# Scatter-add in place of a weighted combine: a mixture-of-experts layer behind latent attention

## The chip, the cores and the metric

The kernel runs on one core of a Trainium2 chip. A core has five engines with queues of their own: TensorE (PE in the profile, its weight loads PEld), VectorE (DVE), ScalarE (ACT), GpSimd (POOL) and SyncE (SP), and 16 DMA engines that move data for all of them. The metric is the device time of one execution in microseconds, as the median of several runs.

## The reference

The input is 8 sequences of 1024 tokens with 256 channels. One attention block with 16 heads comes first, then a layer norm; its result is `x1` (8192 tokens). Then a mixture of 8 experts with two of them chosen for each token, a residual, and two layer norms in a row:

```
gates = softmax(x1 @ gate_w); topw, topi = top_k(gates, 2); topw = topw / sum(topw)
h = gelu(LN(x1 @ w1[e] + b1[e]) * ln1_g[e] + ln1_b[e]);  y[e] = h @ w2[e] + b2[e]
out = LN(sum_e combine[e] * y[e] + x1) * ln_g + ln_b
result = LN(x1 + out)
```

For two chosen experts the normalised weights are 1/(1+exp(d)) and exp(d)/(1+exp(d)), with d the second logit less the first.

## The kernel before

**Attention phase** (`attention_phase`). It is cut into 32 units (8 sequences by 4 groups of heads). Each unit's steps carry places on one axis (the table `PLACES`, 24 places a unit), and every engine runs its own steps sorted by place; so the table is the order of all five queues. At the end of a sequence come the steps that matter here. `STORE` (L410-412) writes the 1024 rows of x1 from the SBUF array `z` to DRAM from SP's queue. `R` is the routing: 22 small DVE steps (`route_step`, L605-650) on 8 columns of tokens, each waiting for the one before; step 12 leaves the difference of the two logits in an array `weight`. `CNT` counts on PE. `SCAT` (L805-811) is 16 indirect DMAs from POOL that write, for every token and choice, a pair of integers into the table `token_of_row`: the token, and the row of `y_rows` that the result goes to.

The last sequence's tail runs in a block of its own together with the loading and splitting of the expert weights. There DVE works out, from the counts, the table of tiles (which expert, which first row), and at its end both gate weights of all tokens (L945-949, with an exponential on ACT, L902).

**Expert phase** (`expert_phase`). There are 136 tiles of 128 rows. All engines run a software pipeline over the tile number k. SP loads the table rows of a tile into `tok` (16 slots). POOL's loop has three steps (L1011-1029): the gather of x1 rows for tile k+6 (L1017), the power -0.5 of the variance for tile k+2 (L1023), and the scatter of the results of tile k-2 (L1028), which puts each row, unweighted, into its own row of `y_rows`. PE transposes, multiplies by w1 and w2 in split precision, ACT applies the gelu and copies the result out of PSUM (L1118), DVE does the normalisation. Rows that pad a tile gather token 0 and scatter to rows of their own behind the results.

**Combine phase** (`combine_phase`). There are 16 groups of 4 tiles of 128 tokens. SP loads three arrays for each group, x1 and the two results y0 and y1, in three rotating buffers each, and stores the output (L1218-1230). ACT builds for each tile two 128x128 diagonal matrices that hold the gate weights (L1337). PE makes f = x1 + w0 y0 + w1 y1 with one identity product and two diagonal ones (L1243, L1245), and x1 + ln_b in a second set (L1254, L1255). DVE takes moments of f, makes 1/sqrt from ACT's square root by a reciprocal and one Newton step (`invert`), forms v = (f - mean) rstd g + (x1 + b) in two passes (L1289, L1295), takes moments of v; ACT applies the last norm (L1354).

## Time and profile before

| what | value |
| --- | --- |
| runs | 2346.51, 2357.85 and 2376.85 us; median 2357.85 |
| span of the profiled execution | 2336.8 us (9.7 below the lowest run shown) |
| busy share of the span | PE 90%, DVE 74%, ACT 58%, POOL 56% |
| expert phase | 1665 to 2172 us of the span, 136 tiles |
| combine phase | 2172 to 2337 us of the span, 16 groups |
| mean granted TensorE clock | 0.94 of full speed |

The span runs from the first to the last instruction of the core; a run's time also holds what lies before and behind it. Busy shares are averages over phases with different limits, so each phase is read by itself. A row of a timeline or a line gives the duration of one instruction; consecutive instructions of one engine overlap a little, so that the distance between starts is the better measure of a series. "idle before <- X" names who ended the wait before an instruction, and "issue" an idle time in which the profile shows no one waited for.

### The profile page before, as it was taken

How to read it: one execution, taken by the hardware profiler on the slowest of the kernel's cores; microseconds unless marked ns; L12 is line 12 of the kernel's file. 1: busy time of each engine (PE TensorE's matmuls, PEld its weight loads, DVE VectorE, ACT ScalarE, POOL GpSimd, SP SyncE). 2: the span in 40 equal slices, each digit the busy share in tenths (PEclk: the TensorE clock that was granted, in tenths of full speed). 3: DMA queues.
4: the chain of work that ended last, by engine and by line, in shares of the span. 5: the costliest groups of instructions: out<-in, count | busy, mean ns of one | idle time of the engine just before them, and what ended most of it. 6: DMA issues, size and time to landing. Idle time of an engine off the chain costs nothing. (4 is left out here: it accounts for less than half of the span.)

```text
span 2336.8 us, 43530 instructions
## 1 busy us (share of the span) xinstructions
PE 2092.7 (90%) x12268; PEld 1464.7 (63%) x12268; DVE 1721.4 (74%) x4995; ACT 1365.5 (58%) x3316; POOL 1308.8 (56%) x1478
## 2 busy tenths in 40 slices
PE   4898999899899899899999999983399999999698
PEld 3554655555555555465556555642399999999587
DVE  3676687677678668668767767836488888888498
ACT  1265655655565565565555556563288887888454
POOL 2355464654764665666465476454577777777000
PEclk7899998999999999999889899995699999999899
DMA  6556556546565554655654556515122222222575
GB/s 176 127 135 142 118 115 149 126 106 150 127 135 128 135 122 118 156 118 116 149 123 109 140 124 146 115 39 213 26 74 74 76 75 76 74 74 69 182 243 168
DMA packets 190406, 284.46 MB, mean 122 GB/s; under 512 B 54072, under 2 KB 111056, under 8 KB 190032
## 3 DMA queue, kind: packets, MB, share of 16 engines
q1 hardware_dynamic: 168608, 236.43, 42.7%
q0 software_dynamic: 17152, 35.81, 5.0%
q10 hardware_dynamic: 4416, 9.44, 1.1%
q8 instruction: 110, 1.80, 0.3%
q14 instruction: 120, 0.98, 0.1%
HBM read 100.03 MB, written 37.90 MB: 59 GB/s over the span
## 5 line engine op out<-in xcount | busy, mean ns | idle before, releaser
L544 ACT ACTIVATE probs<-scores_T 128x512 f32<-128x512 f32 (+3 forms) x1536 | 654.4, 492 | 243.8 <-PE scores_T L433 240.7
L783 POOL TENSOR_SCALAR_AFFINE_SELECT probs<-probs 128x256 f32<-128x256 f32 x512 | 205.7, 410 | 522.4 <-ACT probs L544 519.4
L492 PE MATMUL ring<-k_stack,q_stack_b 96*128 96x512 f32 (+3 forms) x1024 | 396.3, 429 | 22.1 <-DVE neg_part L691 10.4
L691 DVE TENSOR_REDUCE neg_part<-ring 128x1 f32<-128x512 f32 x512 | 333.6, 685 | 97.6 <-PE ring L492 95.6
L433 PE MATMUL scores_T<-q_stack_b,k_stack 98*128 98x512 f32 (+3 forms) x1024 | 318.1, 387 | 45.4 <-ACT probs L544 44.5
L450 PE MATMUL o_ps<-probs,v_ones 128*17 128x512 f32 (+3 forms) x3072 | 341.8, 518 | 2.1 <-POOL probs L783 1.8
L492 PEld LDWEIGHTS ring<-k_stack,q_stack_b 96*128 96x128 f32 x1024 | 192.3, 196 | 227.4 <-issue 72.6
L696 DVE CUSTOM_DVE_ANT_0 ring<-ring,mask 128x384 f32<-128x384 f32 (+3 forms) x512 | 243.6, 508 | 113.5 <-PE ring L492 111.4
L696 DVE CUSTOM_DVE_ANT_0 ring<-ring,mask,neg_part 128x384 f32<-128x384 f32 (+3 forms) x512 | 260.5, 555 | 63.5 <-PE ring L492 63.3
L1107 ACT ACTIVATE o_sb<-ht_ps,ln_b,ln_g 128x128 f32<-128x128 f32 x544 | 217.9, 450 | 87.1 <-PE ht_ps L1056 86.6
L433 PEld LDWEIGHTS scores_T<-q_stack_b,k_stack 98*128 98x128 f32 x1024 | 186.3, 198 | 99.6 <-ACT probs L544 78.6
L552 ACT ACTIVATE u<-ring,lat_bias 128x512 f32<-128x512 f32 x128 | 88.0, 689 | 190.7 <-PE ring L474 178.5
L474 PE MATMUL ring<-x_hi,lat_w 128*128 128x512 f32 x512 | 188.4, 410 | 8.1 <-DMA lat_w<-lat_split 8.1
L492 PE MATMUL ring<-k_stack,q_stack_a 96*128 96x384 f32 (+3 forms) x512 | 170.9, 367 | 25.5 <-DMA k_stack<-u_rot 20.8
L760 POOL TENSOR_TENSOR u<-u,cos 128x512 f32<-128x512 f32 x126 | 162.2, 1287 | 35.9 <-DMA u_rot<-u 35.6
L1017 POOL DMA_INDIRECT z<-x,tok x136 | 147.5, 1084 | 47.8 <-issue 40.4
L768 POOL TENSOR_TENSOR u<-u,u_rot 128x512 f32<-128x512 f32 x126 | 162.8, 1292 | 9.2
L1068 PE MATMUL y_ps<-w_hi,g_hi 128*128 x544 | 164.9, 303 | 2.2 <-DVE g_lo L1134 1.7
L763 POOL TENSOR_TENSOR u_rot<-u_rot,sin 128x512 f32<-128x512 f32 x126 | 164.7, 1307 | 0.1
L1028 POOL DMA_INDIRECT y_rows<-z,tok x136 | 143.6, 1056 | 30.2 <-issue 28.3
L1068 PE MATMUL y_ps<-w_hi,g_lo 128*128 x544 | 154.2, 283 | 0.0
L1068 PE MATMUL y_ps<-w_lo,g_hi 128*128 x544 | 153.8, 283 | 0.0
(190 smaller groups left out, 4552.8 us busy)
## 6 DMA issues: line engine op xcount, KB each, us to landing
u_rot<-u SPq DMA_DIRECT2D x128, 256.0 KB, 3.7
k_stack<-u_rot SPq DMA_DIRECT2D x128, 256.0 KB, 4.3
lat_w<-lat_split SPq DMA_DIRECT2D x32, 512.0 KB
q_stack_a<-u_rot SPq DMA_DIRECT2D x64, 256.0 KB
q_stack_b<-u_rot SPq DMA_DIRECT2D x64, 256.0 KB
k_stack<-u SPq DMA_DIRECT2D x64, 256.0 KB, 4.7
y<-y_rows SPq DMA_DIRECT2D x32, 512.0 KB, 6.7
x_raw<-in_xT SPq DMA_DIRECT2D x16, 512.0 KB, 5.3
```

The source lines that it names most:

```text
L433: nc.tensor.matmul(sc[(t + j) % 3][:, HALF - w:HALF], k_stack[:, n % 2, h, P * kb:P * kb + P], q_stack[c][:, row_buf(n, c), h, q0 - HALF * ...
L450: last = nc.tensor.matmul(o_ps[32 * h:32 * h + VW, q0 - HALF * c:HALF], v_ones[:, b % 2, kb, HG * g + h, :], probs[:, s % 2, h, cols], sta ...
L474: last = nc.tensor.matmul(out[:], lat_w[:, kc, side, w_, :], a[:, kc, cols], start=i == 0, stop=i == 5)
L492: nc.tensor.matmul(out[:, 0:k1 - k0], q_stack[qb // 4][0:3 * L, row_buf(n, qb // 4), h, P * (qb % 4):P * (qb % 4) + P], k_stack[0:3 * L, n ...
L544: nc.scalar.activation(probs[:, s % 2, h, cols], sc[(t + j) % 3][:, HALF - w:HALF], ACT.Exp).then_inc(exp_done, 1)
L691: nc.vector.tensor_reduce(neg_part[:, n % 2, part_col], src[:], AX_X, ALU.max, negate=True).then_inc(max_taken, 1)
L696: nc.vector.tensor_tensor_reduce(out=src[:, 0:w], in0=src[:, 0:w], in1=consts["mask"][:, HALF - w:HALF], scale=-1.0, scalar=neg_part[:, n ...
L763: ops.tensor_tensor(u_rot[s][:, cols], u_rot[s][:, cols], consts["sin"][:, cols], ALU.mult).then_inc(sin_done[s], 1)
L768: ops.tensor_tensor(u[s][:, cols], u[s][:, cols], u_rot[s][:, cols], ALU.add).then_inc(rope_done[s], 1)
L783: nc.gpsimd.affine_select(both, both, [[0, 2], [1, P]], ALU.is_ge, zero, base=0, channel_multiplier=-1).then_inc(kept, 1)
L1068: nc.tensor.matmul(y_ps[j % 2][:, 0:C], a[j % 2][:, f, :], experts[w][:, bass.ds(e, 1), C * f:C * f + C], start=f == 0 and a is g_hi and w ...
L1107: nc.scalar.activation(g[k % 2][:, f, :], ht_ps[k % 2][:, P * f:P * f + P], ACT.Gelu, bias=experts["ln1_b"][:, f, bass.ds(e, 1)], scale=ex ...
```

## The change

The gate weights are now made in the routing: three more DVE steps (22 to 24) and one ACT step `E` for each sequence. They are put as 32-bit floats beside the token in `token_of_row`, in place of the second integer. x1 is stored twice, into `x1` and into a new array `y_sum` of 8192 + 128 rows. In the expert phase ACT multiplies the result of a tile by the weight while it copies it out of PSUM, and the scatter adds it to the token's row of `y_sum` (`compute_op=ALU.add`); since two tiles can hold the same token, POOL waits for the landing of the scatter of tile j-1 before it issues that of tile j. Padding rows go to 128 spare rows. In the last phase SP loads f (from `y_sum`) and x1, each partition reading 4 KB in one piece; PE only makes x1 + b, in two PSUM sets; ACT normalises f in place; POOL multiplies by g; DVE adds; both inverse roots are POOL powers.

```diff
+            for rows in (x1_rows, y_sum):
+                sp.dma_start(rows[B * T:B * T + P, :], dram["x"][0, 0:P, :]).then_inc(tables_loaded, 16)
...
+    "R": (66.5, 0.375), "E": (72, 0), "CNT": (72.25, 0.375), "SCAT": (77, 3.5)}
...
-                    sp.dma_start(x1_dram[n].rearrange("(tb p) c -> p tb c", p=P), z[:]).then_inc(x1_stored, 16)
+                    for rows in (x1_dram, y_sum):
+                        sp.dma_start(rows[T * n:T * n + T, :].rearrange("(tb p) c -> p tb c", p=P),
+                                     z[:]).then_inc(x1_stored, 16)
...
+                elif kind == "E":
+                    act.wait_ge(routed, R_STEPS * n + R_GAP)
+                    nc.scalar.activation(gap_exp[:], gap[:], ACT.Exp).then_inc(gap_exp_ready, 1)
...
             if i == 12:
-                return nc.vector.tensor_tensor(routes["weight"][:, 1, TB * b:TB * b + TB], top[:, 1, :], top[:, 0, :],
-                                               ALU.subtract)
+                return nc.vector.tensor_tensor(gap[:], top[:, 1, :], top[:, 0, :], ALU.subtract)
...
             if i == 20:
-                return nc.vector.tensor_copy(ids[:], ids_f[:])
-            return nc.vector.tensor_scalar(ids_f[:], ids_f[:], float(T), None, ALU.add)
+                return nc.vector.tensor_copy(ids[:, :, :, 0], ids_f[:].unsqueeze(1).to_broadcast([P, 2, TB]))
+            if i == 21:
+                return nc.vector.tensor_scalar(ids_f[:], ids_f[:], float(T), None, ALU.add)
+            if i == 22:
+                return nc.vector.tensor_scalar(gap_sum[:], gap_exp[:], 1.0, None, ALU.add)
+            if i == 23:
+                return nc.vector.reciprocal(weight[:, 0, :], gap_sum[:])
+            return nc.vector.tensor_tensor(weight[:, 1, :], weight[:, 0, :], gap_exp[:], ALU.mult)
 
...
+                    if i == 22:
+                        dve.wait_ge(gap_exp_ready, n + 1)
...
-                act.wait_ge(routed, R_STEPS * B)
-                nc.scalar.activation(w_tmp[:], routes["weight"][:, 1, :], ACT.Exp).then_inc(diff_exp, 1)
...
-                dve.wait_ge(diff_exp, 1)
-                then(nc.vector.tensor_scalar(w_sum[:], w_tmp[:], 1.0, None, ALU.add))
-                then(nc.vector.reciprocal(routes["weight"][:, 0, :], w_sum[:]))
-                nc.vector.tensor_tensor(routes["weight"][:, 1, :], routes["weight"][:, 0, :], w_tmp[:],
-                                        ALU.mult).then_inc(done, 1)
...
                     pool.wait_ge(y_ready, j + 1)
-                    nc.gpsimd.indirect_dma_start(y_rows, bass.IndirectOffsetOnAxis(tok[:, j % 16, 1:2], 0),
-                                                 y_out[j % 4], None).then_inc(y_stored[j % 4], 16)
+                    if j:
+                        pool.wait_ge(y_stored[(j - 1) % 4], 16 * ((j - 1) // 4 + 1))
+                    nc.gpsimd.indirect_dma_start(y_sum, bass.IndirectOffsetOnAxis(tok[:, j % 16, 0:1], 0),
+                                                 y_out[j % 4], None, compute_op=ALU.add).then_inc(y_stored[j % 4], 16)
...
                     act.wait_ge(y_full, j + 1)
+                    act.wait_ge(tok_loaded[j % 4], 16 * (j // 4 + 1))
                     if j >= 4:
                         act.wait_ge(y_stored[j % 4], 16 * (j // 4))
-                    nc.scalar.activation(y_out[j % 4], y_ps[j % 2][:, 0:C], ACT.Identity).then_inc(y_ready, 1)
+                    nc.scalar.activation(y_out[j % 4], y_ps[j % 2][:, 0:C], ACT.Identity,
+                                         scale=tok[:, j % 16, 1:2].bitcast(F32)).then_inc(y_ready, 1)
...
-        tiles_of = lambda m: m.rearrange("(n t p) c -> n p t c", t=CG, p=P)
+        groups_of = lambda m: m.rearrange("(n p t) c -> n p t c", t=CG, p=P)
...
-            for n in range(n_groups + 3):
+            for n in range(n_groups + 2):
                 if n < n_groups:
                     if n >= 3:
-                        sp.wait_ge(mixed, CG * (n - 2))
+                        sp.wait_ge(scaled, CG * (n - 2))
                         sp.wait_ge(xb_ready, CG * (n - 2))
-                    sp.dma_start(x1[n % 3][:], tiles_of(x1_dram)[n]).then_inc(x1_loaded[n % 3], 16)
-                    for k in range(2):
-                        src = tiles_of(y_rows[B * T * k:B * T * (k + 1), :])[n]
-                        sp.dma_start(y[k][n % 3][:], src).then_inc(y_loaded[n % 3], 16)
-                if n >= 3:
-                    m = n - 3
+                    sp.dma_start(f[n % 3][:], groups_of(y_sum[0:B * T, :])[n]).then_inc(f_loaded[n % 3], 16)
+                    sp.dma_start(x1[n % 3][:], groups_of(x1_rows[0:B * T, :])[n]).then_inc(x1_loaded[n % 3], 16)
+                if n >= 2:
+                    m = n - 2
                     sp.wait_ge(out_ready, CG * (m + 1))
-                    sp.dma_start(tiles_of(out)[m], o[m % 2][:]).then_inc(stored[m % 2], 16)
+                    sp.dma_start(groups_of(out)[m], o[m % 2][:]).then_inc(stored[m % 2], 16)
...
             for n in range(n_groups):
                 pe.wait_ge(x1_loaded[n % 3], 16 * (n // 3 + 1))
-                pe.wait_ge(diag_ready, 2 * CG * (n + 1))
-                pe.wait_ge(y_loaded[n % 3], 16 * 2 * (n // 3 + 1))
-                if n >= 3:
-                    pe.wait_ge(scaled, CG * (n - 2))
+                if n >= 2:
+                    pe.wait_ge(v_done, CG * (n - 1))
                 for t in range(CG):
-                    nc.tensor.matmul(f(n, t), routes["ident"][:], x1[n % 3][:, t, :], start=True, stop=False)
-                    for k in range(2):
-                        last = nc.tensor.matmul(f(n, t), diag[n % 2][:, t, k, :], y[k][n % 3][:, t, :],
-                                                start=False, stop=k == 1)
-                    last.then_inc(mixed, 1)
-                if n == 0:
-                    pe.wait_ge(gb_loaded, 32)
-                    pe.wait_ge(row0_set, 2)
-                if n >= 1:
-                    pe.wait_ge(v_done, CG * n)
-                for t in range(CG):
-                    nc.tensor.matmul(xb(t), routes["ident"][:], x1[n % 3][:, t, :], start=True, stop=False)
-                    nc.tensor.matmul(xb(t), row0[:], b_rep[:], start=False, stop=True).then_inc(xb_ready, 1)
+                    nc.tensor.matmul(xb(n, t), routes["ident"][:], x1[n % 3][:, t, :], start=True, stop=False)
+                    nc.tensor.matmul(xb(n, t), row0[:], b_rep[:], start=False, stop=True).then_inc(xb_ready, 1)
...
+                dve.wait_ge(rstd_done[i], n + 1)
+                nc.vector.scalar_tensor_tensor(out=nmr[:, i, d, :], in0=mv[:, i, d, :, 0], scalar=-1.0,
+                                               in1=rstd[:, i, d, :], op0=ALU.mult, op1=ALU.mult).then_inc(nmr_done[i], 1)
...
             for n in range(n_groups + 1):
                 if n < n_groups:
+                    dve.wait_ge(f_loaded[n % 3], 16 * (n // 3 + 1))
                     if n >= 2:
-                        dve.wait_ge(v_done, CG * (n - 1))
-                        dve.wait_ge(sd_done[0], n)
-                    first(n)
+                        dve.wait_ge(normed, CG * (n - 1))
+                    moments(0, n, f[n % 3])
                 if n >= 1:
-                    third(n - 1)
+                    m = n - 1
+                    if m >= 2:
+                        dve.wait_ge(out_ready, CG * (m - 1))
+                    for t in range(CG):
+                        dve.wait_ge(scaled, CG * m + t + 1)
+                        dve.wait_ge(xb_ready, CG * m + (t // 2 * 2 + 2))
+                        nc.vector.tensor_tensor(v[m % 2][:, t, :], t_g[m % 2][:, t, :], xb(m, t),
+                                                ALU.add).then_inc(v_done, 1)
+                    moments(1, m, v[m % 2])
                 if n < n_groups:
-                    invert(0, n)
+                    shift(0, n)
+                if n >= 1:
+                    shift(1, n - 1)
...
+        @block.gpsimd
+        def _(pool):
+            def root(i, n):
+                d = n % 2
+                pool.wait_ge(ve_done[i], n + 1)
+                nc.gpsimd.tensor_tensor(rstd[:, i, d, :], ve[:, i, d, :], minus_half[:], ALU.pow).then_inc(rstd_done[i], 1)
...
+            for n in range(n_groups + 1):
+                if n < n_groups:
+                    root(0, n)
+                if n >= 1:
+                    root(1, n - 1)
+                if n < n_groups:
                     if n >= 2:
-                        dve.wait_ge(out_ready, CG * (n - 1))
-                    second(n)
+                        pool.wait_ge(v_done, CG * (n - 1))
+                    for t in range(CG):
+                        pool.wait_ge(normed, CG * n + t + 1)
+                        nc.gpsimd.tensor_tensor(t_g[n % 2][:, t, :], f[n % 3][:, t, :], g_rep[:],
+                                                ALU.mult).then_inc(scaled, 1)
...
+                    d = n % 2
+                    act.wait_ge(nmr_done[0], n + 1)
+                    for t in range(CG):
+                        nc.scalar.activation(f[n % 3][:, t, :], f[n % 3][:, t, :], ACT.Identity,
+                                             bias=nmr[:, 0, d, t:t + 1],
+                                             scale=rstd[:, 0, d, t:t + 1]).then_inc(normed, 1)
...
-        "no_token": np.stack([np.zeros(ROWS), 2 * B * T + np.arange(ROWS)], 1).astype(np.int32).reshape(P, ROWS // P, 2),
+        "no_token": np.stack([B * T + np.arange(ROWS) % P, np.zeros(ROWS)], 1).astype(np.int32).reshape(P, ROWS // P, 2),
```

POOL's queue at the end of the expert phase, before and in the change (`z<-x,tok` is the gather, `h_rstd` the power, the third kind the scatter; in brackets the semaphores waited for):

```order
L1017 DMA z<-x,tok 128x256 [waits xt_full,tok_loaded3]
L1023 TENSOR_TENSOR h_rstd<-h_ve,minus_half 128x1 [waits h_ve_done]
L1028 DMA y_rows<-z,tok 83968x256 [waits y_ready]
...
L1023 TENSOR_TENSOR h_rstd<-h_ve,minus_half 128x1 [waits h_ve_done]
L1028 DMA y_rows<-z,tok 83968x256 [waits y_ready] x5
```

```order
L1027 DMA z<-x,tok 128x256 [waits xt_full,tok_loaded3]
L1033 TENSOR_TENSOR h_rstd<-h_ve,minus_half 128x1 [waits h_ve_done]
L1040 DMA y_sum<-z,tok 8320x256 [waits y_stored2,y_ready]
...
L1033 TENSOR_TENSOR h_rstd<-h_ve,minus_half 128x1 [waits h_ve_done]
L1040 DMA y_sum<-z,tok 8320x256 [waits y_stored2,y_ready]
L1040 DMA y_sum<-z,tok 8320x256 [waits y_stored3,y_ready]
L1040 DMA y_sum<-z,tok 8320x256 [waits y_stored0,y_ready]
```

The order is the same; each scatter has gained a wait for the slot of the scatter before it, also in the last five, between which nothing else stands.

SP's queue at the start of the last phase, before and in the change (x_0 to x_2 and y_0 to y_2 are the rotating buffers, `out<-o` is the store of a finished group):

```order
L1223 DMA x_2<-x 128x4x256
L1226 DMA y_2<-y_rows 128x4x256 x2
L1223 DMA x_0<-x 128x4x256 [waits xb_ready,mixed]
L1226 DMA y_0<-y_rows 128x4x256 x2
L1230 DMA out<-o 128x4x256 [waits out_ready]
L1223 DMA x_1<-x 128x4x256 [waits xb_ready,mixed]
```

```order
L1229 DMA f<-y_sum 128x1024
L1230 DMA x_2<-x 128x1024
L1234 DMA out<-o 128x1024 [waits out_ready]
L1229 DMA f<-y_sum 128x1024 [waits xb_ready,c_scaled]
L1230 DMA x_0<-x 128x1024
```

Before, four groups were loaded ahead of the first store; now three are, and the fourth group's load stands behind the store of the first.

## Rows read from the trace of the kernel before

**Rows 1.** Windows: us, busy us of PE, PEld, DVE, ACT, POOL; PEclk, DMA share.

```profile
1665.00:2172.00 507.00, 495.80 (x3400) 449.86 (x3400) 427.54 (x1088) 395.04 (x1089) 382.51 (x408) 0.99 0.25 73
...
2172.00:2337.00 165.00, 140.41 (x640) 122.98 (x640) 130.29 (x562) 77.19 (x225) 0.00 (x0) 0.93 0.66 206
```

**Rows 2.** Timeline of POOL, one tile: start us, duration, operation, idle before it.

```profile
1802.54 1.06 POOL L1028 DMA_INDIRECT y_rows<-z,tok  x1 [0.20 <-issue]
...
1803.91 1.11 POOL L1017 DMA_INDIRECT z<-x,tok  x1 [0.31 <-issue]
...
1805.27 0.68 POOL L1023 TENSOR_TENSOR h_rstd<-h_ve,minus_half 128x1 f32<-128x1 f32 x1 [0.26 <-DVE h_ve L1166]
...
1806.14 1.06 POOL L1028 DMA_INDIRECT y_rows<-z,tok  x1 [0.20 <-issue]
```

**Rows 3.** DMA view, 1802 to 1806 us: busy tenths in 40 slices.

```profile
DMA  0989542420000000000305998201000000000967
```

**Rows 4.** Timeline at the expert phase's start: the first gather and its reader.

```profile
1665.62 0.98 POOL L1017 DMA_INDIRECT z<-x,tok  x1 [7.12 <-DMA tok<-token_of_row]
...
1668.47 0.69 PE L1079 MATMUL xt_ps<-ident,z 128*128 128x128 f32 x2 [34.18 <-DMA z<-x,tok]
```

**Rows 5.** Timeline, final five scatters' first and last, first x1 load.

```profile
2162.55 1.30 POOL L1028 DMA_INDIRECT y_rows<-z,tok  x1 [0.20 <-issue]
...
2169.30 0.96 POOL L1028 DMA_INDIRECT y_rows<-z,tok  x1 [0.88 <-ACT z L1118]
...
2178.02 0.43 SPq L1223 DMA_DIRECT2D x<-x  x1
```

**Rows 6.** DMA issues, whole run: count, KB each, median us to landing.

```profile
y_rows<-z,tok POOLq DMA_INDIRECT x136, 2.5
...
x<-x SPq DMA_DIRECT2D x16, 512.0 KB, 5.5
...
out<-o SPq DMA_DIRECT2D x16, 512.0 KB, 3.3
...
x<-z SPq DMA_DIRECT2D x8, 1024.0 KB, 8.4
```

**Rows 7.** Line L1245 on PE: duration ns min/median/max, first and last start.

```profile
L1245 PE MATMUL f_ps<-y,diag x256: 379/379/634, 2186.3 to 2321.9; 128*128 128x256 f32 x128
```

**Rows 8.** Timeline of SP, combine phase: store, load, next store.

```profile
2240.24 0.38 SPq L1230 DMA_DIRECT2D out<-o  x1
...
2240.74 0.42 SPq L1223 DMA_DIRECT2D x<-x  x1
...
2248.87 0.38 SPq L1230 DMA_DIRECT2D out<-o  x1
```

**Rows 9.** Timeline of DVE and ACT, combine phase.

```profile
2257.54 1.64 DVE L1295 SCALAR_TENSOR_TENSOR v<-v,c_rstd,xb_ps 128x256 f32<-128x256 f32 x4
...
2259.10 1.39 DVE L1266 BATCH_NORM_STATS2 c_stats<-v 128x6 f32<-128x256 f32 x4
...
2260.91 0.76 DVE L1266 BATCH_NORM_STATS2 c_stats<-f_ps 128x6 f32<-128x256 f32 x2
...
2264.04 2.07 ACT L1354 ACTIVATE o<-v,c_nmr,c_rstd 128x256 f32<-128x256 f32 x4 [0.39 <-DVE c_nmr L1304]
```

**Rows 10.** Single lines on DVE and POOL: duration ns min/median/max.

```profile
L1141 DVE TENSOR_TENSOR xe_lo<-xt_ps,xe_hi x136: 414/424/426, 1669.6 to 2154.9; 128x256 fp32r<-128x256 f32 x136
...
L798 POOL TENSOR_TENSOR z_rstd<-z_ve,a_minus_half x8: 1670/1672/1689, 328.8 to 1608.2; 128x8 f32<-128x8 f32 x8
...
L789 POOL TENSOR_TENSOR y_T<-y_T,inv_rep x16: 2350/2364/2390, 220.2 to 1589.4; 128x1024 f32<-128x1024 f32 x16
```

**Rows 11.** Timeline of POOL, the last batch's first token scatter.

```profile
1636.77 1.61 POOL L809 DMA_INDIRECT token_of_row<-ids,slot  x1 [14.41 <-DVE ids_f L650]
```

**Rows 12.** Timeline of SP, first store of x1 and the next DMA issued.

```profile
366.43 0.46 SPq L412 DMA_DIRECT2D x<-z  x1
...
376.56 0.58 SPq L384 DMA_DIRECT2D q_stack_a<-max_hi  x1
```

More of the change, by code:

```diff
@@ L219, in attention_phase @@
         top, best, slot_f, slot, ids_f, ids = (tail[k] for k in ("top", "best", "slot_f", "slot", "ids_f", "ids"))
+        gap, gap_exp, gap_sum = (tail[k] for k in ("gap", "gap_exp", "gap_sum"))
+        weight = ids.bitcast(F32)[:, :, :, 1]
         flat = lambda m: m.rearrange("p t e -> p (t e)")
@@ L1168, in _, with combine_phase @@
                     split_g(k, 1)
-def combine_phase(nc, dram, routes, x1_dram, y_rows, out):
+def combine_phase(nc, dram, routes, x1_rows, y_sum, out):
     with ExitStack() as ctx:
@@ L1178, in combine_phase @@
         n_groups = TILES // CG
-        y = [[sb(f"y{k}_{a}", [P, CG, C]) for a in range(3)] for k in range(2)]
+        f = [sb(f"f_{a}", [P, CG, C]) for a in range(3)]
         x1 = [sb(f"x1_{a}", [P, CG, C]) for a in range(3)]
-        row0 = sb("row0", [P, P])
-        diag = [sb(f"diag_{a}", [P, CG, 2, P]) for a in range(2)]
+        t_g = [sb(f"t_g{a}", [P, CG, C]) for a in range(2)]
         v = [sb(f"v_{a}", [P, CG, C]) for a in range(2)]
         o = [sb(f"o_{a}", [P, CG, C]) for a in range(2)]
+        row0, minus_half = sb("row0", [P, P]), sb("c_minus_half", [P, CG])
         g_rep, b_rep = sb("ln_g_rep", [P, C]), sb("ln_b_rep", [P, C])
@@ L1286, in second @@
-            def second(n):
-                d = n % 2
-                for t in range(CG):
-                    nc.vector.scalar_tensor_tensor(out=v[d][:, t, :], in0=f(n, t), scalar=mv[:, 0, d, t, 0:1],
-                                                   in1=g_rep[:], op0=ALU.subtract, op1=ALU.mult).then_inc(scaled, 1)
-                dve.wait_ge(rstd_done[0], n + 1)
-                dve.wait_ge(xb_ready, CG * n + CG)
-                for t in range(CG):
-                    dve.wait_ge(scaled, CG * n + t + 1)
-                    nc.vector.scalar_tensor_tensor(out=v[d][:, t, :], in0=v[d][:, t, :],
-                                                   scalar=rstd[:, 0, d, t:t + 1], in1=xb(t),
-                                                   op0=ALU.mult, op1=ALU.add).then_inc(v_done, 1)
-                moments(1, n, lambda t: v[d][:, t, :], v_done)
@@ L1325, in _ @@
         @block.scalar
         def _(act):
-            def root(i, n):
-                act.wait_ge(ve_done[i], n + 1)
-                nc.scalar.activation(sd[:, i, :], ve[:, i, :], ACT.Sqrt).then_inc(sd_done[i], 1)
-            def diagonals(n):
-                if n >= 2:
-                    act.wait_ge(mixed, CG * (n - 1))
-                for t in range(CG):
-                    for k in range(2):
-                        j = CG * n + t
-                        nc.scalar.activation(diag[n % 2][:, t, k, :], routes["ident"][:], ACT.Identity,
-                                             scale=routes["weight"][:, k, j:j + 1]).then_inc(diag_ready, 1)
@@ L1400, in build @@
             wts, consts, xs = attention_weights(attention, nc, routes, tail)
[L1401 to L1405 removed]
+            weight_phase(nc, dram, wts, consts, lat, token_of_row, x1, y_sum, xs)
+            experts = attention_phase(nc, dram, wts, consts, xs, lat, inv, x1, y_sum, token_of_row, routes, tail,
+                                      attention, ffn)
+            expert_phase(nc, experts, routes, tail, x1, token_of_row, y_sum)
+        combine_phase(nc, dram, routes, x1, y_sum, out.rearrange("b t c -> (b t) c"))
 def ffn_layouts(a):
```

121 lines of the change are left out of this document (44 added, 77 removed).

## Prediction

> **What bounds the kernel now.** I read the busy shares by phase first, then for each phase the view that shows what repeats in it. The expert phase takes 507 us for 136 tiles of 128 rows, with PE busy 496 of them; the last phase takes 165 us, PE busy 140, DVE 130, POOL not at all [rows 1]. These are the two phases that the change rewrites. The attention before them is touched by a few small steps.
>
> In the expert phase one tile takes 3.60 us, from one scatter on POOL to the next [rows 2]. The reader should see that POOL's cycle is nearly closed: scatter 1.06, gap 0.31, gather 1.11, wait 0.25, power 0.68, gap 0.19. So PE sets the pace, but POOL has only the 0.25 us in which it waits for DVE, plus whatever lead the power has over its reader. A scatter lands 2.5 us after its issue [rows 6]. The DMA slices of the same stretch show why: the instruction of 1802.54 ends at 1803.60, and its packets run from about 1804.1 to 1804.9 [rows 3], 0.8 us in which 16 engines move 128 rows. At present nobody waits for that landing.
>
> In the last phase one group of four tiles takes 8.63 us, from store to store [rows 8]. Its 40 PE instructions of 379 ns [rows 7] overlap and fill that time exactly, and the chain that ended last runs on PE's matmuls. DVE is close behind.
>
> **The change, part by part.** I sum against the profiled execution, whose span of 2336.8 us lies 9.7 us under the lowest of the three runs shown and 21.0 us under their median; I carry the difference over to the median of 2357.85.
>
> *Last phase.* PE drops from 40 to 16 instructions a group, 3.5 us at the same rate, and would still fit at half the clock (6.9 us) because its result is wanted a whole iteration after x1 lands. DVE loses both scaled sums and both Newton inversions. What stays per group: two sets of moments, each 1.81 us from the first bn_stats to the next instruction [rows 9]; four additions, which I take at 1.5 us, between the 1.56 us of four fused operations there and four of 0.42 us that overlap [rows 10]; one wait for POOL's power on four columns. No row has four columns: one takes 0.68 and eight take 1.67 [rows 2, 10], so about 1.1, and I allow 0.1 for each of the two hand-overs, 1.3 us. With the small product behind it: 1.81 + 1.81 + 1.5 + 1.3 + 0.2 = 6.6 us. POOL has two powers and four products of 256 columns, together as many columns as the one of 1024 that takes 2.36 us [rows 10]; with starts some 3.0, in all 5.2 us: under 6.6, and it runs while DVE does the next group's moments. ACT has two sets of four at 2.07 us [rows 9], 4.2 us.
>
> But the sum of DVE is not the period. SP issues in program order, and the load of group n now stands behind the store of group n-3, where it stood behind that of n-4. ACT finishes group n-1's output about 3.1 us after DVE's iteration n ends (2.07 for the first scaling, which starts 1.2 early, then 2.07). SP issues the store, 0.5 later the load [rows 8], and such a load, right behind a store, lands 5.5 us after issue [rows 6]. The load so released is read two DVE iterations later. Two periods therefore hold 3.1 + 0.5 + 5.5 + 6.6 = 15.7 us: 7.85 a group. Laid out from the first load: the load 4.5, first iteration 3.3, second 7.2, third 6.6, the fourth ends at 30.7, the sixteenth six double periods later at 124.9, the last DVE work 6.4, ACT 2.2, store and end 3.4: 137 us. Before it is 159 us from the first x1 load at 2178.0 [rows 5] to the span's end at 2336.8. **Worth 22 us.** If the loads keep ahead, the period is 6.6 and it is worth 39 us; if they land like the y loads (6.7 us, my choice of a bad case from the phase's slowest transfers), 14 us.
>
> *Expert phase, steady state.* Four things are added: the scatter reads its destination and adds; POOL waits for the landing of the scatter before; ACT takes its scale from the table (the same activation, and ACT waits for PE every tile, so nothing); ACT waits for a table row loaded six tiles ahead, also nothing. The destination being one array of 8320 rows costs nothing that a row shows. What is behind POOL's new wait: the gather for six tiles later, and the power that DVE's normalisation needs. The price is the landing L of an accumulating scatter, which the trace does not have. It cannot be under 2.5 us, because a plain scatter is part of it. From above: a gather, which reads DRAM, is usable 2.85 us after its issue [rows 4]; gather and scatter in full sequence with one descriptor generation are 2.85 + 2.5 - 1.06 = 4.3 us, and with two 5.35 us. I take 3.3: the plain 2.5, with the 0.8 us of packets doubled, since each engine reads two operands; nearest is the plain scatter's row, of the same rows, size and queue. POOL can restart a scatter every L + 0.1, so up to L = 3.5 the tile stays at 3.60 us and the wait is free, hidden by gather and power. Above it every 0.1 us costs 0.1 x 132 = 13 us.
>
> The Trainium skill, "Collectives: The Full Stack", section "The bandwidth ceiling", says that adding in the DMA engine costs no cycles, but needs two source reads and so halves the rate; by it the landing is the 3.3 us above, and no run here shows it yet. "DMA: Bandwidth & Descriptors", section "Rules for kernel authors", speaks against the change: an accumulate reads its destination and writes it later, so each must wait for the earlier one's semaphore. No trace here shows a lost addition; what the wait costs is the first rival.
>
> *Expert phase, end.* Here the wait is not free. The last five scatters start between 2162.55 and 2169.30 [rows 5], since by then POOL has a backlog that it works off with no gather between. Now they start at least 3.4 us apart: 2162.55 + 4 x 3.4 = 2176.15. **Costs 6.9 us, and 0.8 for the later landing of the last.** (At L = 2.5, 3.7 in all; at 4.3, 12.6.)
>
> *Routing.* Three more DVE steps a batch; I allow 0.26 us each, with the wait for the step before. In seven batches they lie between reductions of a phase that PE sets, and the scatters that they hold back have until the next batch. ACT's exponential waits for the gap, taken just before it in both orders; its place is in an idle stretch of ACT. In the last batch POOL waits for the last step [rows 11], so the end of routing moves by 3 x 0.26 = **0.8 us**; the block ends with these scatters. The weights' three steps at the end of the table chain go; they lay beside these scatters, so nothing is gained.
>
> *Second store of x1.* Eight times 1 MB. The first store is issued at 366.43 and lands 8.4 us later, at 374.8, and SP issues nothing until 376.56 [rows 6, 12]. The second fits mostly in that hole: nothing taken, up to 4 us over eight batches kept as an end. The two 128 KB fills at the start lie beside it.
>
> Sum: -22 + 7.7 + 0.8 = -13.5 us: 2344 us from the median, -0.6%.
>
> **The rivals.**
>
> *The added landing decides (slower).* L comes out nearer to a read and a write in sequence: 4.3 us. Then a tile takes 4.4, and 0.8 x 132 = 106 us come on top, with 4.9 more at the end: 2344 + 111 = 2455 us. It decides from L = 3.5, only 0.2 above my value, and POOL's instruction may grow too, as it has more descriptors to write; it has 0.25 us of room before its own cycle passes 3.60. For it: no slack to speak of, and a DRAM read must end before its write starts. Against it: packets of one scatter overlap across 16 engines, and a DRAM read costs little more than the SBUF read (2.85 against 2.5). With two generations' worth, 5.35, it is 1.85 x 132 + 10 on top, 2598 us. At 3.9 it is some 55, 2399 us, still no change that can be told.
>
> *The loads keep ahead in the last phase.* Rows are now 4 KB in one piece and only two transfers go with each store. Then 39 us instead of 22: 2327 us.
>
> *The last phase does not gain.* The loads behind the store take 9 us in place of 5.5, two periods hold 19.2, and 13 x 1.75 = 22 us are gone again: 2366 us.
>
> **How the numbers follow.** Forecast 0.38. Landing over 3.5: 0.49, of which 0.14 with L up to 3.9, 0.22 around 4.3 and 0.13 well above. Loads ahead 0.08, half of that lower still with a lucky landing and runs. No gain in the last phase 0.05. Two per cent of 2357.85 is 47 us, about what a measurement of this kernel can tell: faster than 2311 asks for more than the whole best case (2323: 39 less 3.7 and 0.8) and gets 0.04; within 2%, 0.38 + 0.14 + 0.04 + 0.05 = 0.61; slower 0.35. The forecast's own range is 2323 to 2360. The range given goes from 2318 to 2490: below lies 0.04, above some 0.15, most of the landings well above 4.3.
>
> **What would show it.** Right: scatters still 3.60 us apart in mid-phase, landing at 3.0 to 3.5, PE at 0.98 busy there; the last five 3.3 or more apart; the last phase's stores 7.5 to 8 us apart in pairs, with DVE waiting for f. Wrong: POOL waiting before each scatter and PE idle for the transposes of h_norm; a scatter instruction over 1.3 us; stores 6.6 us apart; or DVE waiting for POOL's products.

## The result and the profile after

The change made the kernel slower: 2508.94 us as the median of its runs (2503.72 to 2516.67) against 2363.43 for the kernel before on the same chip, a ratio of 1.0627 (95% interval 1.0584 to 1.0671). The forecast was 2344, its range ended at 2490.

The profiled execution of the change spans 2507.9 us, 171.1 more than the 2336.8 before. I split both spans at two events, the first gather of the expert phase and the first load of the last phase:

| stretch | before | change | difference |
| --- | --- | --- | --- |
| up to the first gather | 1665.6 | 1694.1 | +28.5 |
| expert phase, to the first load | 512.4 | 685.8 | +173.4 |
| last phase, to the end of the span | 158.8 | 128.0 | -30.8 |

The windows of the change, for the expert and the last phase (columns as in [rows 1]):

```profile
1694.00:2380.00 686.00, 584.76 (x3400) 462.85 (x3400) 432.82 (x1091) 406.61 (x1089) 436.15 (x408) 0.97 0.34 54
2380.00:2507.00 127.00, 75.30 (x256) 59.16 (x256) 92.21 (x384) 64.75 (x128) 76.22 (x96) 0.80 0.57 201
```

PE has the same 3400 instructions in the expert phase as in [rows 1], but is busy 585 of 686 us where it was busy 496 of 507: it no longer sets the pace. POOL's timeline answers to [rows 2]:

```profile
1801.53 1.63 POOL L1040 DMA_INDIRECT y_sum<-z,tok  x1 [1.21 <-DMA y_sum<-z,tok]
1803.46 0.99 POOL L1027 DMA_INDIRECT z<-x,tok  x1 [0.30 <-issue]
1804.47 0.59 POOL L1033 TENSOR_TENSOR h_rstd<-h_ve,minus_half 128x1 f32<-128x1 f32 x1
1806.10 1.63 POOL L1040 DMA_INDIRECT y_sum<-z,tok  x1 [1.04 <-DMA y_sum<-z,tok]
```

Three things differ. The scatter takes 1.63 us in place of 1.06. Before it POOL is idle over 1 us, ended by the landing of the scatter before. And the power has no idle time in front of it: it comes late. The mean distance from one scatter to the next is 4.83 us (median 4.66); before it was 3.55. 1.28 x 135 = 173 us, the loss of the whole phase.

Who pays is in the waits of the change from 1720 to 2330 us (engine and line, what it waited for: us in total, times, longest):

```profile
DVE h_norm L1169 <- POOL h_rstd L1033: 195.6, 125, 3.4
POOL y_sum L1040 <- DMA y_sum<-z,tok: 149.3, 119, 3.1
```

DVE's normalisation of h waits for the power that stands behind the scatter in POOL's queue, and PE, whose transposes read what DVE normalises, waits for DVE. The landing, from the DMA issues of the whole run, against the 2.5, 5.5 and 3.3 of [rows 6]:

```profile
y_sum<-z,tok POOLq DMA_INDIRECT x136, 3.9
...
f<-y_sum SPq DMA_DIRECT2D x16, 512.0 KB, 4.8
x<-x SPq DMA_DIRECT2D x16, 512.0 KB, 5.7
out<-o SPq DMA_DIRECT2D x16, 512.0 KB, 3.0
```

The DMA slices between the two scatters above (1801.5 to 1806.1, 0.115 us each) answer to [rows 3]. The first burst of high digits is the adding scatter, the second the gather:

```profile
DMA  0000121000000000000996978997420699092000
```

The scatter starts at 1801.53, its packets run from slice 19 (1803.7) to slice 30 (1805.0), 1.3 us. A plain scatter's take 0.5 us as the median of the trace of before. The one in [rows 3] had a last packet on its own until 1805.1 and landed after 3.0 us, so that the prediction's reading of 0.8 is no typical value. The queue that indirect DMAs use shows it over the whole run, of before and then of the change (packets, MB, share of 16 engines' span):

```profile
q0 software_dynamic: 17152, 35.81, 5.0%
```

```profile
q0 software_dynamic: 30208, 35.81, 8.9%
```

The bytes are the same, but 13056 packets more, 96 a scatter. Their time grew from 0.050 x 2336.8 to 0.089 x 2507.9 us per engine: 106 us more over 136 scatters, **0.8 us each**. For one scatter alone, with nothing beside it on the queue, first a plain one of the wait-only kernel below (2199.8 to 2202.2 us), then one of the change (2365.9 to 2369.9 us):

```profile
q0 software_dynamic: 48, 0.13, 15.4%
```

```profile
q0 software_dynamic: 144, 0.13, 28.0%
```

That is 0.154 x 2.4 = 0.37 us per engine against 0.28 x 4.0 = 1.12: three times as much, not twice. The plain scatter's data go in 32 packets of 4096 bytes, the adding one's in 128 of 1024. How much of the time is due to the smaller packets and how much to the addition no run separates.

### The profile page after: what moved, and what is told of

Its sections match the earlier page's. It is cut to its first block and busy times, and to the rows that moved or that the text cites. A ratio compares the mean times of both kernels' runs of the same rounds, so it can differ in the third digit from the quotient of the medians.

```text
span 2507.9 us, 42787 instructions
## 1 busy us (share of the span) xinstructions
PE 2155.0 (86%) x11884; PEld 1434.5 (57%) x11884; DVE 1702.5 (68%) x4841; ACT 1366.2 (54%) x3226; POOL 1437.2 (57%) x1574
## 5 line engine op out<-in xcount | busy, mean ns | idle before, releaser
L500 PE MATMUL ring<-k_stack,q_stack_b 96*128 96x512 f32 (+3 forms) x1024 | 406.7, 440 | 20.8 <-DVE neg_part L707 12.7
L441 PE MATMUL scores_T<-q_stack_b,k_stack 98*128 98x512 f32 (+3 forms) x1024 | 330.0, 400 | 34.4 <-ACT probs L552 33.7
L458 PE MATMUL o_ps<-probs,v_ones 128*17 128x512 f32 (+3 forms) x3072 | 351.5, 532 | 1.5 <-POOL probs L801 1.5
L500 PEld LDWEIGHTS ring<-k_stack,q_stack_b 96*128 96x128 f32 x1024 | 198.1, 202 | 234.8 <-issue 81.4
L1040 POOL DMA_INDIRECT y_sum<-z,tok x136 | 221.9, 1632 | 187.2 <-DMA y_sum<-z,tok 168.7
L441 PEld LDWEIGHTS scores_T<-q_stack_b,k_stack 98*128 98x128 f32 x1024 | 195.2, 208 | 91.8 <-ACT probs L552 67.7
L1169 DVE TENSOR_SCALAR h_norm<-h_norm,h_mv,h_rstd 128x512 f32<-128x512 f32 x136 | 74.5, 548 | 202.1 <-POOL h_rstd L1033 202.1
L1080 PE MATMUL y_ps<-w_hi,g_hi 128*128 x544 | 179.8, 331 | 15.9 <-issue 12.5
L1027 POOL DMA_INDIRECT z<-x,tok x136 | 134.6, 990 | 48.7 <-issue 40.4
```

Of the source, the lines that this page charges most:

```text
L441: nc.tensor.matmul(sc[(t + j) % 3][:, HALF - w:HALF], k_stack[:, n % 2, h, P * kb:P * kb + P], q_stack[c][:, row_buf(n, c), h, q0 - HALF * ...
L458: last = nc.tensor.matmul(o_ps[32 * h:32 * h + VW, q0 - HALF * c:HALF], v_ones[:, b % 2, kb, HG * g + h, :], probs[:, s % 2, h, cols], sta ...
L500: nc.tensor.matmul(out[:, 0:k1 - k0], q_stack[qb // 4][0:3 * L, row_buf(n, qb // 4), h, P * (qb % 4):P * (qb % 4) + P], k_stack[0:3 * L, n ...
L1040: nc.gpsimd.indirect_dma_start(y_sum, bass.IndirectOffsetOnAxis(tok[:, j % 16, 0:1], 0), y_out[j % 4], None, compute_op=ALU.add).then_inc( ...
L1080: nc.tensor.matmul(y_ps[j % 2][:, 0:C], a[j % 2][:, f, :], experts[w][:, bass.ds(e, 1), C * f:C * f + C], start=f == 0 and a is g_hi and w ...
```

## The experiments

In every experiment the expert phase is measured from the first gather to the first load of the last phase, the last phase from there to the end of the span. Ratios are to the kernel before, run on the same chip. Phases, distances and landings are read from one profiled execution each. The kernel with the addition taken out and those with four and with two arrays leave part of the result out; their times answer a question, and none of them could stand for the change. **Theory A:** an adding scatter takes so long to land that waiting for it in series sets the tile. **Rival B:** the adding scatter itself is too dear, whoever waits. **Rival C:** the wait alone is what costs.

**The addition taken out, the wait kept.**

```diff
                     nc.gpsimd.indirect_dma_start(y_sum, bass.IndirectOffsetOnAxis(tok[:, j % 16, 0:1], 0),
-                                                 y_out[j % 4], None, compute_op=ALU.add).then_inc(y_stored[j % 4], 16)
+                                                 y_out[j % 4], None).then_inc(y_stored[j % 4], 16)
```

> The changed kernel with one thing taken out: the scatter no longer adds, it overwrites the token's row of y_sum, so the output leaves out x1 and one of the two results. The wait for the scatter before stays, and so does everything else. Theory A (the landing of an adding scatter, waited for in series, sets the tile): without the addition the instruction takes 1.06 us and lands 2.5 us after issue, the wait ends before POOL needs it, tiles are 3.55 to 3.60 us apart again in place of 4.83, 1.25 x 135 = 169 us go: about 2340 us, 0.98 to 0.995 of the kernel before, the last five scatters 2.6 to 3.6 apart. Rival C (the wait itself, its place in POOL's queue, is what costs): tiles stay over 4.3 us apart and the time over 2440. Rival D (the weighted copy or the table read by ACT costs): tiles between 3.7 and 4.8, PE waiting for ACT.

Measured: 2344.65 us, ratio 0.9946 (0.9913 to 0.9978); expert phase 523.5 us, scatters 3.58 us apart (median), instruction 1.06 and landing 2.5 us. One argument of one instruction accounts for 162 of the 173 us; the other 11 are near the 12 that the wait alone costs in the next experiment. Rival D of the expectation (the weighted copy or the table) falls with it: the weighted copy and the routing are in this kernel too.

**The wait alone, in the kernel before.**

```diff
                     pool.wait_ge(y_ready, j + 1)
+                    if j:
+                        pool.wait_ge(y_stored[(j - 1) % 4], 16 * ((j - 1) // 4 + 1))
                     nc.gpsimd.indirect_dma_start(y_rows, bass.IndirectOffsetOnAxis(tok[:, j % 16, 1:2], 0),
```

> The kernel before with one thing added: POOL waits for the landing of the scatter of tile j-1 before it issues that of tile j. Theory A: a plain scatter lands 2.5 us after issue, 1.1 us before the next is due, so mid-phase tiles stay 3.60 us apart and only the last five scatters move, to 2.6 or more apart: 0 to +5 us, 1.000 to 1.002. Rival C (the wait itself costs): 0.1 us or more per tile, +13 us or more, over 1.005.

Measured: 2373.17 us, ratio 1.0068 (1.0032 to 1.0103); expert phase 524.8 us, 12.4 more than before. The wait is not free: my 0 to +5 was too low, and 1.0068 lies beyond the 1.005 that I had set as the mark of rival C. But the distance of most tiles is unchanged (median 3.58), so it is no steady cost of each tile, and 12 us are not 173. Half of it is the end: the last five scatters span 13.0 us in place of 6.8. The last scatters on POOL:

```profile
2193.42 1.01 POOL L1030 DMA_INDIRECT y_rows<-z,tok  x1 [2.20 <-DMA y_rows<-z,tok]
2196.61 0.96 POOL L1030 DMA_INDIRECT y_rows<-z,tok  x1 [2.18 <-ACT z L1120]
2199.76 0.96 POOL L1030 DMA_INDIRECT y_rows<-z,tok  x1 [2.18 <-DMA y_rows<-z,tok]
2202.90 0.96 POOL L1030 DMA_INDIRECT y_rows<-z,tok  x1 [2.19 <-DMA y_rows<-z,tok]
```

Nothing else stands between them, so their distance is the loop itself: 3.14 us. The landing of these five has a median of 2.4 us. **From a landing to the start of the next scatter 0.7 us go by**, where the prediction had 0.1. (The second row names ACT; ACT had long been done, since the distance is that of its neighbours.) The other half comes in mid-phase. Nine times between 1780 and 2098 us the next scatter is 4.4 to 6.0 us behind. In six of these cases the scatter before landed late, after 3.9 to 4.5 us, such as here (landing 4.5):

```profile
2037.77 1.32 POOL L1030 DMA_INDIRECT y_rows<-z,tok  x1 [0.35 <-issue]
...
2043.02 1.30 POOL L1030 DMA_INDIRECT y_rows<-z,tok  x1 [2.06 <-ACT z L1120]
```

In one it took 3.3 us. In the other two it landed on time (2.6 and 2.5 us), ACT's copy had been done for over 7 us, and POOL still started the next scatter only 3.4 and 3.5 us after the landing; what held it there stays open:

```profile
1896.88 1.06 POOL L1030 DMA_INDIRECT y_rows<-z,tok  x1 [0.36 <-issue]
...
1902.87 1.06 POOL L1030 DMA_INDIRECT y_rows<-z,tok  x1 [3.05 <-ACT z L1120]
```

The kernel before has landings up to 4.5 us in the same stretch, and does not notice.

**Four arrays: the addition kept, the wait in series gone.**

```diff
-                    if j:
-                        pool.wait_ge(y_stored[(j - 1) % 4], 16 * ((j - 1) // 4 + 1))
-                    nc.gpsimd.indirect_dma_start(y_sum, bass.IndirectOffsetOnAxis(tok[:, j % 16, 0:1], 0),
+                    if j >= 4:
+                        pool.wait_ge(y_stored[j % 4], 16 * (j // 4))
+                    nc.gpsimd.indirect_dma_start(([y_sum] + others)[j % 4], bass.IndirectOffsetOnAxis(tok[:, j % 16, 0:1], 0),
                                                  y_out[j % 4], None, compute_op=ALU.add).then_inc(y_stored[j % 4], 16)
```

> The changed kernel with the addition kept, but tile j adds into one of four arrays (j modulo 4), so a scatter waits only for the one four tiles before; the last phase reads one of the four arrays, so the output leaves out what went to the other three. Theory A (landing and serial wait): the 1.25 us wait before each scatter goes, and POOL's own cycle is left, 1.63 + 0.30 + 0.99 + 0.02 + 0.59 + 0.3 = 3.83 us, which is over the 3.55 to 3.60 of PE: tiles 3.8 to 3.95 apart, (4.83 - 3.87) x 135 = 130 us less than the change: 2380 us, 1.005 to 1.015 of the kernel before. Rival B (the adding transfer itself is the bottleneck, engines or queue, whoever waits): landings stretch as scatters overlap and tiles stay over 4.4 us apart, over 2450 us. Third possibility: POOL's 1.63 us shortens when nothing competes, then 3.60 and 2345.

Measured: 2363.7 us, ratio 1.0027 (1.0 to 1.0054), under the 1.005 to 1.015 that I expected; the distance came out as expected: expert phase 547.6 us, scatters 3.79 us apart (median; 3.89 as the mean of the middle). This kernel makes all 136 additions, with a median landing of 3.8 to 3.9 us as in the change, and loses 35 us in the phase where the change loses 173. Its POOL timeline is closed:

```profile
1902.52 1.63 POOL L1040 DMA_INDIRECT y_other<-z,tok  x1 [0.19 <-issue]
1904.45 1.05 POOL L1027 DMA_INDIRECT z<-x,tok  x1 [0.30 <-issue]
1905.53 0.58 POOL L1033 TENSOR_TENSOR h_rstd<-h_ve,minus_half 128x1 f32<-128x1 f32 x1
1906.30 1.89 POOL L1040 DMA_INDIRECT y_other<-z,tok  x1 [0.19 <-issue]
1908.50 1.00 POOL L1027 DMA_INDIRECT z<-x,tok  x1 [0.30 <-issue]
```

No idle time but the gaps between instructions: POOL's own work, 3.8 to 4.0 us a tile, is over PE's 3.60. Rival B, in the form that POOL's longer instruction closes its own cycle, is worth these 35 us; the wait for the landing is worth the other 138 (685.8 - 547.6). The kernel below that moves only the last phase's stores took 676.3 in this phase, with the same code in it, so 129 to 138.

**Two arrays**, even and odd tiles, with the wait for the scatter two tiles before.

```diff
-                    if j:
-                        pool.wait_ge(y_stored[(j - 1) % 4], 16 * ((j - 1) // 4 + 1))
-                    nc.gpsimd.indirect_dma_start(y_sum, bass.IndirectOffsetOnAxis(tok[:, j % 16, 0:1], 0),
+                    if j >= 2:
+                        pool.wait_ge(y_stored[(j - 2) % 4], 16 * ((j - 2) // 4 + 1))
+                    nc.gpsimd.indirect_dma_start(([y_sum] + others)[j % 2], bass.IndirectOffsetOnAxis(tok[:, j % 16, 0:1], 0),
```

> The changed kernel with two arrays in place of one: even tiles add into y_sum, odd tiles into a second array, and a scatter waits for the landing of the one two tiles before; the last phase reads only y_sum, so the output leaves out what went to the second array. Theory A': the series loop of an adding scatter is 4.4 us (the distance of the last scatters of the change), which two arrays spread over two tiles, 2.2 a tile; POOL's own cycle binds as with four arrays: 3.80 us a tile, expert phase 546 to 552 us, 2358 to 2370 us, 1.000 to 1.006 of the kernel before. Rival B' (adding scatters that overlap slow each other, or the late landings of 5 to 6 us reach through two tiles): over 4.0 us a tile, expert phase over 575, over 1.012.

Measured: 2371.51 us, ratio 1.0046 (1.0004 to 1.0088); expert phase 549.5 us, 3.79 us a tile (median). As expected: two chains of 4.4 us beside each other need 2.2 us a tile, and POOL's own cycle binds. The late landings no longer show either, because a landing may now take two tiles; in the middle no distance is over 4.0 us.

**The stores of the last phase one group later.**

```diff
-            for n in range(n_groups + 2):
+            for n in range(n_groups + 3):
...
-                if n >= 2:
-                    m = n - 2
+                if n >= 3:
+                    m = n - 3
```

> The changed kernel with the last phase's stores moved one group later in SP's queue (n-3 in place of n-2), as in the kernel before; nothing else. Theory (the load behind the store closes the loop of two groups): period from 7.15 to what DVE needs, 6.6 to 6.8 us; the last phase from 128 us to 121 to 124. Rival (engines set the period, the load arrives in time): 7.15 stays, 127 to 129 us.

Measured in a single execution, so without an interval: last phase 124.1 us against 128.0 in the change. SP's stores, of the change and then of this kernel:

```profile
2412.39 0.34 SPq L1234 DMA_DIRECT2D out<-o  x1
...
2419.57 0.34 SPq L1234 DMA_DIRECT2D out<-o  x1
...
2426.55 0.34 SPq L1234 DMA_DIRECT2D out<-o  x1
```

```profile
2405.49 0.34 SPq L1234 DMA_DIRECT2D out<-o  x1
...
2412.47 0.34 SPq L1234 DMA_DIRECT2D out<-o  x1
...
2419.43 0.34 SPq L1234 DMA_DIRECT2D out<-o  x1
```

In the change the period wanders between 6.97 and 7.9 us; here it is 6.97 group after group. So 6.97 is what DVE needs (forecast 6.6), and the load behind the store costs 0.27 on average. Theory and rival each hold in part: the load does close the loop at times, but DVE sets most of the period. The theory's 6.6 to 6.8 was missed for DVE's part:

```profile
2422.07 0.17 DVE L1262 TENSOR_SCALAR c_ve<-c_mv 128x4 f32<-128x4 f32 x1
2422.15 0.16 DVE L1267 SCALAR_TENSOR_TENSOR c_nmr<-c_mv,c_rstd 128x4 f32<-128x4 f32 x1
2423.36 0.68 DVE L1267 SCALAR_TENSOR_TENSOR c_nmr<-c_mv,c_rstd 128x4 f32<-128x4 f32 x1 [1.05 <-POOL c_rstd L1300]
2423.97 1.39 DVE L1257 BATCH_NORM_STATS2 c_stats<-f 128x6 f32<-128x256 f32 x4
```

The row at 2423.36 waits for POOL's power, 1.05 us of idle DVE, and then takes 0.68 us for 4 columns where its twin takes 0.16.

**The second store of x1, in the kernel before.**

```diff
-                    sp.dma_start(x1_dram[n].rearrange("(tb p) c -> p tb c", p=P), z[:]).then_inc(x1_stored, 16)
+                    for rows in (x1_dram, x1_copy):
+                        sp.dma_start(rows[n].rearrange("(tb p) c -> p tb c", p=P), z[:]).then_inc(x1_stored, 16)
```

> The kernel before with x1 stored a second time, into an array that nobody reads, right behind the first store; nothing else. Forecast: it fits mostly in the hole of SP's queue, 0 to +4 us over eight sequences, 1.000 to 1.002. Rival: each delays the stacks that SP issues next by its 0.5 us of issue and up to the 9 us in which both stores share the DMA engines, 8 x 1 to 2 us: +8 to +16, over 1.003.

Measured: 2360.65 us, ratio 1.0008 (0.9978 to 1.0037). No cost that can be measured.

**Weights at routing, no addition.** The same table with a third integer, plain scatter, last phase with identities for the diagonals.

```diff
-                    nc.scalar.activation(y_out[j % 4], y_ps[j % 2][:, 0:C], ACT.Identity).then_inc(y_ready, 1)
+                    nc.scalar.activation(y_out[j % 4], y_ps[j % 2][:, 0:C], ACT.Identity,
+                                         scale=tok[:, j % 16, 2:3].bitcast(F32)).then_inc(y_ready, 1)
...
-                        last = nc.tensor.matmul(f(n, t), diag[n % 2][:, t, k, :], y[k][n % 3][:, t, :],
+                        last = nc.tensor.matmul(f(n, t), routes["ident"][:], y[k][n % 3][:, t, :],
```

> The kernel before with the gate weights made at routing (three more DVE steps, one ACT step, a third integer in the table) and applied by ACT as it copies a tile out of PSUM; the scatter is plain, into a row of its own for each result, and the last phase adds x1, y0 and y1 by three identity products, without diagonals. No wait added. Forecast: routing +1 us, expert phase 512 to 515 us with 3.60 a tile, last phase unchanged at 158 to 159 because its 40 PE instructions remain: 0 to +3 us, 1.000 to 1.002. Rival D (the change's routing or weighting costs): attention and expert phase over 10 us longer, over 1.004.

Measured: 2353.28 us, ratio 0.9983 (0.9956 to 1.001); expert phase 514.4, last phase 158.8 us. The routing's new steps and the weighted copy cost nothing that can be measured.

**The parts that pay, together:** the kernel just described, with the change's last phase fitted to three loads in runs of 4 KB.

```diff
-                    nc.tensor.matmul(xb(t), row0[:], b_rep[:], start=False, stop=True).then_inc(xb_ready, 1)
+                    nc.tensor.matmul(xb(n, t), tail["ones"][:], b_rows[:], start=False, stop=True).then_inc(xb_ready, 1)
...
+                        nc.scalar.activation(fn[n % 2][:, t, :], f(n, t), ACT.Identity,
+                                             bias=nmr[:, 0, d, t:t + 1],
+                                             scale=rstd[:, 0, d, t:t + 1]).then_inc(normed, 1)
...
+                        nc.gpsimd.tensor_tensor(t_g[n % 2][:, t, :], fn[n % 2][:, t, :], g_rep[:],
+                                                ALU.mult).then_inc(scaled, 1)
```

> The same weighting at routing and plain scatter, with the change's last phase fitted to three loads: x1, y0, y1 in runs of 4 KB, PE adds them in PSUM and makes x1 + b with one 16-bit product in place of two 32-bit passes, ACT normalises out of PSUM, POOL multiplies by g and makes both powers, DVE adds; stores one group later than in the change. Forecast: PE's 36 instructions a group at 8.63/40 = 0.216 each with the short ones less give 7.4 us, DVE 6.6 to 7.15: period 7.2 to 7.6, last phase 136 to 141 us in place of 159, expert phase as before: 15 to 22 us less than the kernel before, 0.991 to 0.994. Rival (three loads of 512 KB behind a store bind now): period 8.6, no gain, 1.000.

Measured: 2338.26 us, ratio 0.9933 (0.9905 to 0.9961): 20 us less than the kernel before, of which the last phase gives 15. The expert phase takes 514.1, the last 143.6 us (3 over my bound) with a period of 7.36 (median; 7.47 as the mean). PE binds there now, busy 98.9 us of the 100 from 2200 to 2300; DVE waits for it:

```profile
2233.47 0.76 DVE L1269 BATCH_NORM_STATS2 c_stats<-f_ps 128x6 f32<-128x256 f32 x2 [0.48 <-PE f_ps L1249]
...
2241.58 0.76 DVE L1269 BATCH_NORM_STATS2 c_stats<-f_ps 128x6 f32<-128x256 f32 x2 [1.24 <-PE f_ps L1249]
```

## Why the prediction was wrong

**The step that failed is the steady state of the expert phase**, costed at nothing; the phase, with its end, took 173 us more. The mechanism was named (the first rival, with its place and the waits that would show it), and the choice against it rested on two terms, both too small.

*The landing.* I took 3.3 us: the plain 2.5 with 0.8 us of packets doubled. From the start of POOL's instruction to the landing there are four parts, as medians of the trace: the instruction, the time to the first data packet, the packets, and the time from the last of them to the landing. For a plain scatter they are 1.06 + 0.57 + 0.51 + 0.36 = 2.50 us, for an adding one 1.63 + 0.57 + 1.33 + 0.35 = 3.88. The packets thus added the 0.8 us that I had put down for them, but by luck: they were 0.5 us long and not 0.8, and they grew to 2.6 times and did not double (doubled, they would have given 3.0). What the sum lacked was the instruction, which grew by 0.57. I had written that the instruction might grow, and put it into a rival instead of into the sum.

*The hand-over.* "POOL can restart a scatter every L + 0.1": the wait-only kernel shows 3.14 for a landing of 2.4, and the end of the change 4.36 for 3.6 to 3.7:

```profile
2361.47 1.55 POOL L1040 DMA_INDIRECT y_sum<-z,tok  x1 [2.85 <-DMA y_sum<-z,tok]
2365.83 1.55 POOL L1040 DMA_INDIRECT y_sum<-z,tok  x1 [2.81 <-DMA y_sum<-z,tok]
2370.19 1.55 POOL L1040 DMA_INDIRECT y_sum<-z,tok  x1 [2.81 <-DMA y_sum<-z,tok]
```

So it is L + 0.7, and 0.78 in mid-phase (the median of the change), and the threshold lay at L = 2.8 to 2.9 and not at 3.5. Even my own 3.3 would have given 4.0 us a tile and 53 us more. With the true landing it is 3.88 + 0.78 = 4.66, the measured median. That the rival's 4.4 came near is partly luck: its landing of 4.3 was 0.4 too long, its hand-over of 0.1 nearly 0.7 too short. Its 2455 us for the whole was still 54 too low.

*What no part had.* The mean is 4.83 and not 4.66, because 18 distances in the change are 5.3 to 6.7 us, and a chain without slack never makes up for a delay. In 13 of them the scatter landed late (4.5 to 5.9 us); in five it took 3.8 to 4.4 us and POOL started the next one 1.7 to 2.1 us after the landing. (4.83 - 4.66) x 135 = 23 us. With 4.66 alone the change would stand some 23 us lower, inside the range given; without a term for such delays the range was too short above.

*Expert end.* Forecast 7.7 us. The last five scatters span 18.6 us in place of 6.8 [rows 5]; by then the chain is the whole phase, and it is counted in the 173.

*Last phase.* Right in direction, 22 us forecast, 31 measured; the mechanism held in small part. The loop of two periods through the load was to set 7.85 us a group. The period came out at 7.24, and 6.97 of it are DVE's. DVE took 6.97 and not 6.6, but f landed in 4.8 us and not 5.5 (4 KB in one piece, two loads), so that the load behind the store was nearly in time: moving the store gave 4 us and not the 17 between my two cases. PE, POOL and ACT were under DVE, as written.

*Routing and second store.* Forecast 0.8 and 0. The 28.5 us in the table before the first gather are no cost of the change. The kernel with only the wait added has the attention phase of the kernel before, unchanged, and its first gather stands at 1686.8; the kernel with a plain scatter has the change's attention phase, and its first gather stands at 1666.5. From 30 to 1590 us, of the kernel before and of the change:

```profile
30.00:1590.00 1560.00, 1423.70 (x8079) 864.44 (x8079) 1100.00 (x3224) 873.86 (x1976) 885.15 (x1041) 0.94 0.55 125
```

```profile
30.00:1590.00 1560.00, 1450.66 (x8003) 880.77 (x8003) 1113.46 (x3243) 866.95 (x1962) 874.38 (x1027) 0.92 0.56 129
```

PE did fewer instructions in more busy time, at a granted clock of 0.92 against 0.94. The profile before was of the kernel's lowest run, and the medians differ by 145.5 us: 173.4 - 30.8 leaves some 3 for all the rest.

The Trainium skill, "Collectives: The Full Stack", section "The bandwidth ceiling", has two source reads halve the rate. The trace shows a larger factor here: 0.37 us of packet time per engine became 1.12, and the packets of a scatter last 1.33 us in place of 0.51. The Trainium skill, "DMA: Bandwidth & Descriptors", section "Rules for kernel authors", asks for the wait between accumulates into one place. The kernels with four and with two arrays, where overlapping additions go to different arrays, put the price of keeping to it here at 138 and 136 us (129 and 127 by the lower of the two phases with a single array). They do not pay for bringing the arrays together again: the last phase reads only one.

## What to carry to other kernels

Before a transfer that nobody waits for becomes one that is waited for in series, compare its whole loop with the tile: the issuing instruction as it will be, the packets, and the time from landing to the next start, which was 0.7 us here. A series wait also takes in every late landing, so a loop that just fits by its median already loses. Where the loop does not fit, spread it over two destinations, whose joining was not measured here, or keep plain writes to rows of their own, and take from such a change the parts that do not hang on it (here the last phase, 15 us of the 20 by which the last kernel is faster).

## What the runs showed of the hardware

- An adding scatter of 128 rows of 1 KB takes 1.63 us on POOL against 1.06 for a plain one, sends 96 packets more for the same bytes (128 of 1024 bytes in place of 32 of 4096, beside 16 small ones in both), and lands in 3.9 against 2.5 us.
- From the landing of a scatter to the start of the next one that waits for it POOL takes 0.7 to 0.8 us.
- With two arrays and with four every second scatter takes 1.89 us on POOL in place of 1.63. It is not the second array as such: with four, the scatters into the third take 1.63 like those into `y_sum`, those into the second and fourth 1.89. Why was not settled. With two arrays:

```profile
L1040 POOL DMA_INDIRECT y_other<-z,tok x68 | 126.1, 1855 | 15.0 <-issue 12.4 <-DMA y_other<-z,tok 1.2 <-ACT z L1131 1.1
L1040 POOL DMA_INDIRECT y_sum<-z,tok x68 | 110.8, 1630 | 12.9 <-issue 12.3 <-PE xt_ps L1091 0.4 <-ACT z L1131 0.3
```

- Now and then a scatter lands 1 to 2 us late: up to 4.6 in the kernels with a plain one, 5.9 in the change. All six that landed in 3.9 us or more in the wait-only kernel had a 16 KB transfer on queue 8, of the kind "instruction", beside their packets; 32 of its 136 scatters had one, and none of the other 104 landed later than 2.9. In the change it is 11 of the 13 late ones. No run takes such transfers away, so that this is a coincidence in time and not a cause shown.
